# Smaller weight rows, unread padding and fewer full-precision passes in the routed expert blocks of a scan and mixture-of-experts kernel

## Chip, core and metric

The kernel runs on one core of a Trainium2 chip. The metric is the device time of one execution in microseconds (us); the median of three runs of the kernel before is 881.7 us (881.13 to 884.68). A core has TensorE (PE: matmuls), VectorE (DVE), ScalarE (ACT), GpSimd (POOL) and SyncE (SP), which here only issues transfers, and 16 DMA engines that they share. Each engine runs its own list of instructions in order; semaphores order them between engines.

## The reference

```python
x = x + xattn(ctx, layernorm(x))             # 2048 tokens, 512 features: a selective state-space scan
h = layernorm(x)
aff = sigmoid(h @ wa)                        # 16 experts
topk_p, topk_i = top_k(aff, 2);  topk_p /= sum(topk_p)
expert(e, h) = (gelu(h @ g[e] + gb[e]) * (h @ w1[e] + b1[e])) @ w2[e] + b2[e]   # 512 -> 256 -> 512
routed = sum over the two chosen e of topk_p * expert(e, h)
shared = sum of two experts that every token goes through
out = x + h + shared + routed
```

All is fp32. The change concerns `routed` alone.

## The kernel before

Up to about 406 us the kernel computes the projections and the scan, then, to about 596 us, gates, layer norms, the router and the two shared experts. The routed experts follow.

The 4096 pairs of token and expert are sorted by expert into NBLK = 47 blocks of 128 rows, and an expert's last block is filled up with padding rows. Blocks that no expert needs come first; they hold padding alone. The tables of the blocks lie in SBUF: `ids` (the tokens of its rows; padding has the numbers 2048 to 2175, which are spare rows of the scratch tensor `xn_dram` and of `out`), `row_w` (the routing weight of each row, 0 for padding), `blk_e` (the expert), `blk_load` (1 if the block has another expert than the block before it), `blk_slot` (which of four weight slots).

A block j is worked on by all engines, in a pipeline with a ring of four:
- SyncE, `load_up(j)` and `load_down(j)` (L387 to L402): reads expert, condition and slot from the tables into registers (L389 to L391) and issues a conditional DMA (L392) of 1 MB (up and gate weights, 128 rows of 8 KB) or 512 KB (down weights, rows of 4 KB). If the condition is 0, nothing is moved, but the semaphore is still raised. The order is load_down(j), load_up(j + 3), for j from 4 on. load_up(j + 3) first waits until the up product of block j - 1 is done, load_down(j) until the down product of block j - 4 is.
- GpSimd: `fetch` (L599) gathers the 128 token rows of a block from `xn_dram`, in the order of `ids`; later the indirect scatter-add of the block's result into `out` (L631). Scatter j waits until scatter j - 2 has landed, and, if a new expert begins, until scatter j - 1 has too.
- TensorE: turns the tokens (L1760), `up` (L1763 to L1776), turns the gated product (L1782), `down` (L1785 to L1795). `up` contracts 512 features in KC = 4 chunks of 128. KSPLIT = 2 of them are computed as three single-pass matmuls on values split into head and rest (L1446 to L1448), the others in full fp32 (L1774). Its order in step j is up(j + 1), turn_hidden(j), turn_tokens(j + 3), down(j - 1).
- ScalarE: `weight_head(j + 2)` (L906) and the heads and copies of the turned tokens (L898, L899), the Gelu (L910), the copy of the turned product (L915), and `block_result(j - 2)` (L919), which multiplies the result by `row_w`.
- VectorE: bias of the up product (L1385), rest of the tokens (L1377), bias of the result of block j - 2 (L1399), gated product (L1391), rest of the weights of block j + 2 (L1372).

The heads and rests lie in `acc_again`, the memory of `acc`, whose tiles hold the shared result until they are stored to `out` (L588). The biases of all experts are loaded in four transfers of 2 MB (L413 to L416), behind the first four up and four down loads.

Of the kernel before, what the change touches and what calls it, by code (L numbers as in the profile page):

```python
# [18 lines left out]
F32 = mybir.dt.float32  # L19
F32R = mybir.dt.float32r  # L20
I32 = mybir.dt.int32
U32 = mybir.dt.uint32
ALU = mybir.AluOpType
# [3 lines left out]
P = 128  # L27
# [16 lines left out]
AHEAD = 3  # L44
KSPLIT = 2
GROUP = NT // 2
# [6 lines left out]
def bass_xattn_scan_moe_kernel(nc, x, ctx_t, in_proj_t, conv_w, conv_b, x_proj_t, dt_proj_t, dt_b,  # L53
# [6 lines left out]
    with ExitStack() as ctx:  # L60
# [160 lines left out]
        with ExitStack() as listing:  # L221
            blk_val = listing.enter_context(nc.sbuf_tensor("blk_val", [P, 2, GROUP, 2 * NBLK], F32))
        blk_val_again = sb("blk_val_again", [P, 2 * GROUP * 2 * NBLK])
        AHEAD_OF_DOWN = (2 * SH * FC, 2 * SH * FC + 1)
        blk_val_all = blk_val[:].rearrange("p a g j -> p (a g j)")

# [6 lines left out]

        half_i = sb("half_i", [P, 2 * ((NBLK + 3) // 2)], I32)
        half_f = sb("half_f", [P, 2 * ((NBLK + 3) // 2)])
# [50 lines left out]
        uph_made upr_made xgr_made up_0 up_1 up_2 up_3 down_0 down_1 down_2 down_3 xg_0 xg_1 xg_2 xg_3 xgt_ready xgt_copied h_ready  # L286
        hb_ready hg_ready hy_ready hyt_ready hyt_copied o_ready yb_ready y_ready y_even y_odd
        """.split()
# [30 lines left out]
        def _(sp):  # L319
# [67 lines left out]

            def load(weights, r_weights, loaded, j, r):
                e = sp.value_load(blk_e[0:1, ds(j, 1)], min_val=0, max_val=E - 1)  # L389
                new = sp.value_load(blk_load[0:1, ds(j, 1)], min_val=0, max_val=1)  # L390
                slot_j = sp.value_load(blk_slot[0:1, ds(j, 1)], min_val=0, max_val=SLOTS - 1)  # L391
                sp.dma_start(weights[:, ds(slot_j, 1)], r_weights[ds(e, 1)].rearrange("e p n -> p e n"), cond=new).then_inc(s[f"{loaded}_{r}"], 16)  # L392

            def load_up(j, r):
                if not isinstance(j, int) or j >= SLOTS:
                    wait_apart(sp, s["h_ready"], j - SLOTS + 1)
                load(up_w, r_up, "up", j, r)

            def load_down(j, r):
                if not isinstance(j, int) or j >= SLOTS:  # L400
                    wait_apart(sp, s["o_ready"], j - SLOTS + 1)
                load(down_w, r_down, "down", j, r)  # L402

# [26 lines left out]
        def _(pool):  # L430
# [14 lines left out]
            pool.iota(tok_i[:], [[P, NT]], base=0, channel_multiplier=1).then_inc(s["consts_made"], 1)  # L445
            pool.iota(half_i[:], [[16, (NBLK + 3) // 2], [0, 2]], base=-16, channel_multiplier=0).then_inc(s["consts_made"], 1)
            pool.tensor_copy(iota_f[:], row_i[:, 0:48]).then_inc(s["consts_made"], 1)
            pool.wait_ge(s["consts_made"], 6)

            pool.dma_start(xn_dram[T:T + P, :], no_rows).then_inc(s["pad_stored"], 16)  # L450
            pool.dma_start(out[T:T + P, :], no_rows).then_inc(s["pad_stored"], 16)
            pool.tensor_copy(tok_f[:], tok_i[:]).then_inc(s["consts_made"], 1)
            pool.tensor_copy(half_f[:], half_i[:]).then_inc(s["consts_made"], 1)
            pool.wait_ge(s["consts_made"], 8)
# [131 lines left out]
            def store_base(t):  # L586
                pool.wait_ge(s["so_added"], t + 1)
                pool.dma_start(out[t * P:(t + 1) * P, :], acc[:, t]).then_inc(s["early_stored" if t < NT // 2 else "late_stored"], 16)  # L588

# [8 lines left out]
            def fetch(j):  # L598
                pool.indirect_dma_start(out=xg[:, j % RING], out_offset=None, in_=xn_dram,  # L599
                                        in_offset=bass.IndirectOffsetOnAxis(ids[:, j:j + 1], 0)).then_inc(  # L600
                                            s[f"xg_{j % RING}"], 16)
# [10 lines left out]
            for i in range(NBLK + BEHIND):  # L612
                if FIRST <= i and i + RING < NBLK:
                    pool.wait_ge(s["xgt_ready"], i + 1)
                    fetch(i + RING)
                j = i - BEHIND
                if j < 0:
                    continue
                if j == 0:
                    pool.wait_ge(s["early_stored"], 16 * NT // 2)  # L620
                    pool.wait_ge(s["late_stored"], 16 * NT // 2)
                pool.wait_ge(s["y_ready"], j + 1)
                if j >= 2:
                    pool.wait_ge(s["y_odd" if j % 2 else "y_even"], 16 * (j // 2))
                if 0 < j < 3:
                    pool.wait_ge(s["y_even" if j % 2 else "y_odd"], 16)
                elif j >= 3:

                    landed = pool.value_load(blk_wait[0:1, j:j + 1], min_val=16, max_val=16 * NBLK)
                    wait_apart(pool, s["y_even" if j % 2 else "y_odd"], landed)  # L630
                pool.indirect_dma_start(out=out, out_offset=bass.IndirectOffsetOnAxis(ids[:, j:j + 1], 0),  # L631
                                        in_=y_sb[j % RING], in_offset=None, compute_op=ALU.add).then_inc(
                                            s["y_odd" if j % 2 else "y_even"], 16)
# [5 lines left out]
        def _(act):  # L639
# [255 lines left out]
            def turn_tokens(j, half):  # L895
                act.wait_ge(s["xgt_ready"], j + 1)
                since(act, s["h_ready"], j - 1)
                act.copy(one_pass(xgt_head[:, half]), ps[:, 4 + half, 0:KSPLIT * P]).then_inc(s["xgt_copied"], 1)  # L898
                act.copy(xgt[:, half], ps[:, 4 + half, KSPLIT * P:D]).then_inc(s["xgt_copied"], 1)  # L899

            def weight_head(j, r, round_):

                slot_j = act.value_load(blk_slot[0:1, ds(j, 1)], min_val=0, max_val=SLOTS - 1)
                act.wait_ge(s[f"up_{r}"], 16 * (round_ + 1))
                since(act, s["h_ready"], j - 1)
                act.copy(one_pass(up_head[:, r % 2]), up_weights(slot_j, 0, KSPLIT)).then_inc(s["uph_made"], 1)  # L906

# [8 lines left out]

            def block_result(j, r):
                act.wait_ge(s["yb_ready"], j + 1)
                act.activation(y_sb[r], y_sb[r], ACT.Copy, scale=row_w[:, ds(j, 1)]).then_inc(s["y_ready"], 1)  # L919

            def step(j, round_, r):

                if not isinstance(j, int) or j + 2 < NBLK:
                    weight_head(j + 2, (r + 2) % RING, round_ + (r + 2) // RING)
                    turn_tokens(j + 2, r % 2)
                hidden_gate(j, r % 2)
                if not isinstance(j, int) or j >= 4:
                    block_result(j - 2, (r - 2) % RING)
                turn_hidden(j, r % 2)
                if isinstance(j, int) and j == 3:  # L930
                    block_result(0, 0)
                    block_result(1, 1)

# [3 lines left out]
            turn_tokens(1, 1)  # L937
            act.wait_ge(s["early_stored"], 16 * NT // 2)
            weight_head(0, 0, 0)
# [6 lines left out]
            for j in range((NBLK - 2) // RING * RING, NBLK):  # L946
                step(j, j // RING, j % RING)
            for j in range(NBLK - 2, NBLK):
                block_result(j, j % RING)


        @block.vector
        def _(dve):
# [433 lines left out]
            def hidden(j, half):  # L1387
                since(dve, s["hyt_ready"], j - 1)
                dve.wait_ge(s["hg_ready"], j + 1)
                dve.wait_ge(s["hb_ready"], j + 1)  # L1390
                dve.tensor_tensor(hy[:, half], hg[:, half], hb[:, half, F:2 * F], ALU.mult).then_inc(s["hy_ready"], 1)  # L1391

            def add_bias(j, r, round_):

                e = expert_of(j)
                if not isinstance(j, int) or j >= RING:
                    wait_apart(dve, s["y_odd" if r % 2 else "y_even"], 16 * (RING // 2 * round_ + r // 2 - 1))
                dve.wait_ge(s["o_ready"], j + 1)
                dve.tensor_tensor(y_sb[r], ps[:, 6 + r % 2], tile(b2_all, e), ALU.add).then_inc(s["yb_ready"], 1)  # L1399

            def step(j, round_, r):
# [3 lines left out]
                if not isinstance(j, int) or 1 < j < NBLK - 1:  # L1405
                    token_rest(j + 1, (r + 1) % 2)
                if not isinstance(j, int) or j >= 4:
                    add_bias(j - 2, (r - 2) % RING, round_ + (r - 2) // RING)
                hidden(j, r % 2)
                if isinstance(j, int) and j == 3:  # L1410
# [27 lines left out]
        def _(pe):  # L1438
# [346 lines left out]
            def down(j, r, round_):  # L1785
                slot_j = pe.value_load(blk_slot[0:1, ds(j, 1)], min_val=0, max_val=SLOTS - 1)
                pe.wait_ge(s["hyt_copied"], j + 1)
                pe.wait_ge(s[f"down_{r}"], 16 * (round_ + 1))
                if isinstance(j, int) and j == 0:
                    pe.wait_ge(s["so_added"], NT)  # L1790
                since(pe, s["yb_ready"], j - 1)
                for fc in range(FC):
# [90 lines left out]
```

## Time and profile before

| | us |
|---|---|
| median of 3 runs | 881.7 |
| profiled execution | 884.4 |
| its span | 882.3 |
| TensorE busy | 783.9 |
| VectorE busy | 660.8 |
| ScalarE busy | 557.5 |
| GpSimd busy | 550.5 |
| scan until | about 406 |
| routed blocks, first full-precision up product to the end | 596.4 to 882.3 |

Busy time leaves out register, branch, semaphore and DMA-issuing instructions: SyncE has no such row, and its load has to be read from the list of its issues and from the instructions of one line. The chain of work that ended last is followed back from the last instruction, at each step to what released it. A wait for several semaphores is put down to the one that came last. Line numbers (L392) are those of the kernel before.

### The profile page before, as it was taken

How to read it: one execution, taken by the hardware profiler on the slowest of the kernel's cores; microseconds unless marked ns; L12 is line 12 of the kernel's file. 1: busy time of each engine (PE TensorE's matmuls, PEld its weight loads, DVE VectorE, ACT ScalarE, POOL GpSimd, SP SyncE). 2: the span in 40 equal slices, each digit the busy share in tenths (PEclk: the TensorE clock that was granted, in tenths of full speed). 3: DMA queues.
4: the chain of work that ended last, by engine and by line, in shares of the span. 5: the costliest groups of instructions: out<-in, count | busy, mean ns of one | idle time of the engine just before them, and what ended most of it. 6: DMA issues, size and time to landing. Idle time of an engine off the chain costs nothing.

```text
span 882.3 us, 16042 instructions
## 1 busy us (share of the span) xinstructions
PE 783.9 (89%) x4358; PEld 589.2 (67%) x4359; DVE 660.8 (75%) x859; ACT 557.5 (63%) x931; POOL 550.5 (62%) x347
## 2 busy tenths in 40 slices
PE   6963799999999988997899999999999998999992
PEld 3622688888888878886777778886555554555551
DVE  4999999999999998999586759544655555556651
ACT  3896899999999999994333431024555554545541
POOL 9651399989999999997815560211444543546532
PEclk9975899999999999999799999999999999999996
DMA  6010311212141122101220121366577867678753
GB/s 182 1 55 0 108 52 58 60 49 61 50 155 49 54 61 92 59 14 49 95 96 1 49 102 42 129 253 275 121 163 226 235 175 223 154 211 205 180 143 48
DMA packets 35384, 95.57 MB, mean 108 GB/s; under 512 B 7760, under 2 KB 8272, under 8 KB 32000
## 3 DMA queue, kind: packets, MB, share of 16 engines
q1 hardware_dynamic: 23360, 65.50, 21.6%
q0 software_dynamic: 11968, 29.37, 15.6%
q8 instruction: 30, 0.49, 0.2%
q14 instruction: 26, 0.21, 0.1%
HBM read 122.24 MB, written 21.36 MB: 163 GB/s over the span
## 4 chain that ended last, share of the span: by engine, by line
PE 43%; DMA 17%; DVE 17%; POOL 9%; issue 7%; ACT 5%; POOLq 1%; DVEq 0%; SPq 0%; ACTq 0%
DVE r L1060 12%; DMA out<-sb_sb,ids 9%; DMA out<-sg,ids 8%; PE ps L1446 6%; PE ps L1448 6%; PE ps L1447 6%; PE ps L1549 5%; POOL r L526 5%; PE ps L1572 5%; PE ps L1550 3%; PE ps L1774 3%; PE ps L1793 2%; DVE r L963 1%; POOL r L599 1%; ACT mem L765 1%
## 5 line engine op out<-in xcount | busy, mean ns | idle before, releaser
L526 POOL TENSOR_TENSOR r<-r,mem 128x1024 f32<-128x1024 f32 x126 | 295.4, 2380 | 34.8 <-DVE r L1060 34.2
L1060 DVE TENSOR_TENSOR_SCAN r<-r,ps 128x1024 f32<-128x1024 f32 x128 | 286.7, 2276 | 9.7 <-issue 9.1
L750 ACT ACTIVATE r<-mem,nega 128x511 f32<-128x511 f32 x256 | 166.9, 714 | 1.8 <-DVE r L1060 1.7
L1549 PE MATMUL ps<-ident,mem 128*128 128x128 f32 x768 | 130.3, 279 | 28.4 <-DVE r L1060 21.7
L1572 PE MATMUL ps<-ident,r 128*128 128x128 f32 x1024 | 132.6, 273 | 1.5 <-POOL r L526 1.3
L765 ACT ACTIVATE mem<-mem,b_turned 128x512 f32<-128x512 f32 x192 | 124.7, 715 | 8.7 <-PE ps L1550 8.3
L1549 PEld LDWEIGHTS ps<-ident,mem 128*128 128x128 f32 x768 | 87.2, 142 | 53.8 <-issue 52.8
L1572 PEld LDWEIGHTS ps<-ident,r 128*128 128x128 f32 x1024 | 115.8, 141 | 2.3 <-POOL r L526 1.8
L1550 PE MATMUL ps<-mem 128*128 128x128 f32 x512 | 99.7, 277 | 0.0
L1793 PE MATMUL ps<-mem 128*128 x188 | 92.2, 615 | 1.8 <-ACT mem L915 1.0
L1446 PE MATMUL ps<-split 128*128 128x512 f32 x216 | 88.2, 408 | 4.8 <-DVE split L1134 2.3
L1774 PE MATMUL ps<-r,picked 128*128 x188 | 88.3, 592 | 0.0
L631 POOL DMA_INDIRECT out<-sg,ids x24 | 40.6, 1693 | 72.4 <-DMA out<-sg,ids 29.6
L1448 PE MATMUL ps<-split 128*128 128x512 f32 x216 | 85.0, 394 | 0.0
L1447 PE MATMUL ps<-split 128*128 128x512 f32 x216 | 85.0, 394 | 0.0
L1550 PEld LDWEIGHTS ps<-mem 128*128 128x128 f32 x512 | 78.1, 193 | 0.0
L631 POOL DMA_INDIRECT out<-sb_sb,ids x23 | 38.1, 1656 | 61.4 <-DMA out<-sb_sb,ids 32.0
L1372 DVE TENSOR_TENSOR acc_again<-r,acc_again 128x1024 fp32r<-128x1024 f32 x47 | 57.6, 1225 | 20.4 <-issue 20.0
L906 ACT CAST acc_again<-r 128x1024 fp32r x47 | 49.1, 1046 | 32.7 <-issue 21.9
L599 POOL DMA_INDIRECT r<-xn_scratch,ids x47 | 49.6, 1055 | 31.8 <-PE ps L1760 19.2
L915 ACT COPY mem<-ps 128x256 f32<-128x256 f32 x47 | 17.5, 372 | 67.9 <-PE ps L1782 67.7
L825 ACT ACTIVATE sg<-ps,sbg_sb 128x512 f32<-128x512 f32 x16 | 11.0, 688 | 71.0 <-PE ps L1448 71.0
(205 smaller groups left out, 1304.8 us busy)
## 6 DMA issues: line engine op xcount, KB each, us to landing
r<-in_r_up SPq DMA_DIRECT2D x47, 1024.0 KB
mem<-in_r_down SPq DMA_DIRECT2D x47, 512.0 KB
mem<-cm_rows SPq DMA_DIRECT2D x64, 256.0 KB, 3.3
mem<-in_r_b SPq DMA_DIRECT2D x4, 2048.0 KB, 15.1
out<-acc POOLq DMA_DIRECT2D x17, 256.0 KB, 3.2
r<-in_x SPq DMA_DIRECT2D x4, 1024.0 KB, 4.9
xn_scratch<-r SPq DMA_DIRECT2D x16, 256.0 KB, 2.7
mem<-in_ctx_t SPq DMA_DIRECT2D x4, 512.0 KB, 7.7
```

Of the source, the lines that this page charges most:

```text
L526: pool.tensor_tensor(state[:, k % 2, ec:ec + 2], state[:, k % 2, ec:ec + 2], c, ALU.mult).then_inc(s["weighed"], 1)
L750: act.activation(decay[:, k % 2, ec, 1:L], delta[:, b, ec, 1:L], ACT.Exp, scale=nega[:, ec, n:n + 1]).then_inc(s["decay_ready"], 1)
L765: act.activation(dbu_t[:, k % 2, lt], du_t[:, t], ACT.Copy, scale=b_turned[:, t, k % DS:k % DS + 1]).then_inc(s["dbut_made_a"], 1)
L1060: dve.tensor_tensor_scan(state[:, half, ec:ec + 2].rearrange("p e l -> p (e l)"), decay[:, half, ec:ec + 2].rearrange("p e l -> p (e l)"), ...
L1446: pe.matmul(to, one_pass(l_head), one_pass(r_head), start=(first and i == 0), stop=False)
L1447: pe.matmul(to, one_pass(l_head), one_pass(r_rest), start=False, stop=False)
L1448: mm = pe.matmul(to, one_pass(l_rest), one_pass(r_head), start=False, stop=(last and i == n - 1))
L1549: pe.transpose(ps[:, ec, lt * P:(lt + 1) * P], dbu_t[:, k % 2, lt, ec * P:(ec + 1) * P], ident[:])
L1550: pe.matmul(ps[:, ec, (LT - 1) * P:LT * P], du_t[:, k // DS * LT + LT - 1, ec * P:(ec + 1) * P], b_diag[k % 2], start=True, stop=True).the ...
L1572: mm = pe.matmul(ps[:, Y_BANK + lt, ec * P:(ec + 1) * P], state[:, k % 2, ec, lt * P:(lt + 1) * P], ident[:], is_transpose=True, start=Fal ...
L1774: mm = pe.matmul(ps[:, r % 2], xgt[:, r % 2, (kc - KSPLIT) * P:(kc - KSPLIT + 1) * P], up_weights(slot_j, kc, kc + 1), start=False, stop=( ...
L1793: mm = pe.matmul(ps[:, 6 + r % 2], hyt[:, r % 2, fc * P:(fc + 1) * P], down_weights(slot_j, fc), start=(fc == 0), stop=(fc == FC - 1))
```

## The change

- `load` takes a list of parts: load_up issues four DMAs of one chunk each (128 rows of 2 KB), load_down two (128 rows of 2 KB), all with the same condition, registers and semaphore. Those who wait for the weights wait for 16 x 4 or 16 x 2.
- `fetch` has a bounds check: padding rows are not read, and the rows of `xg` keep what they held.
- VectorE multiplies by `row_w`: the gated product and the bias each take it in a fused operation. `block_result` and its semaphore are gone; the bias add raises `y_ready` itself.
- In VectorE's step the gated product stands before the bias add of block j - 2.
- KSPLIT = 3: three chunks in single passes, one in full fp32. The heads and rests are longer by half.
- ScalarE's first weight head waits until 12 tiles of the shared result are stored, not 8. Some tables share memory.

```diff
-KSPLIT = 2
+KSPLIT = 3
...
-            def load(weights, r_weights, loaded, j, r):
+            def load(parts, loaded, j, r):
+
                 e = sp.value_load(blk_e[0:1, ds(j, 1)], min_val=0, max_val=E - 1)
                 new = sp.value_load(blk_load[0:1, ds(j, 1)], min_val=0, max_val=1)
                 slot_j = sp.value_load(blk_slot[0:1, ds(j, 1)], min_val=0, max_val=SLOTS - 1)
-                sp.dma_start(weights[:, ds(slot_j, 1)], r_weights[ds(e, 1)].rearrange("e p n -> p e n"), cond=new).then_inc(s[f"{loaded}_{r}"], 16)
+                for weights, r_weights in parts:
+                    sp.dma_start(weights[:, ds(slot_j, 1)], r_weights[ds(e, 1)].rearrange("e p n -> p e n"), cond=new).then_inc(s[f"{loaded}_{r}"], 16)
...
-                load(up_w, r_up, "up", j, r)
+                load([(up_w[:, :, kc * 2 * F:(kc + 1) * 2 * F], r_up[:, :, kc * 2 * F:(kc + 1) * 2 * F]) for kc in range(KC)], "up", j, r)
...
-                load(down_w, r_down, "down", j, r)
+                load([(down_w[:, :, fc], r_down[:, :, fc * D:(fc + 1) * D]) for fc in range(FC)], "down", j, r)
...
-                                        in_offset=bass.IndirectOffsetOnAxis(ids[:, j:j + 1], 0)).then_inc(
+                                        in_offset=bass.IndirectOffsetOnAxis(ids[:, j:j + 1], 0),
+                                        bounds_check=T - 1, oob_is_err=False).then_inc(
...
-                act.wait_ge(s[f"up_{r}"], 16 * (round_ + 1))
+                act.wait_ge(s[f"up_{r}"], 16 * KC * (round_ + 1))
...
-            def block_result(j, r):
-                act.wait_ge(s["yb_ready"], j + 1)
-                act.activation(y_sb[r], y_sb[r], ACT.Copy, scale=row_w[:, ds(j, 1)]).then_inc(s["y_ready"], 1)
-
...
-            act.wait_ge(s["early_stored"], 16 * NT // 2)
+            act.wait_ge(s["early_stored"], 16 * (NT - LT))
...
-                dve.tensor_tensor(hy[:, half], hg[:, half], hb[:, half, F:2 * F], ALU.mult).then_inc(s["hy_ready"], 1)
+                dve.scalar_tensor_tensor(out=hy[:, half], in0=hg[:, half], scalar=row_w[:, ds(j, 1)], in1=hb[:, half, F:2 * F],
+                                         op0=ALU.mult, op1=ALU.mult).then_inc(s["hy_ready"], 1)
...
-                dve.tensor_tensor(y_sb[r], ps[:, 6 + r % 2], tile(b2_all, e), ALU.add).then_inc(s["yb_ready"], 1)
+                dve.scalar_tensor_tensor(out=y_sb[r], in0=tile(b2_all, e), scalar=row_w[:, ds(j, 1)], in1=ps[:, 6 + r % 2],
+                                         op0=ALU.mult, op1=ALU.add).then_inc(s["y_ready"], 1)
...
+                hidden(j, r % 2)
                 if not isinstance(j, int) or j >= 4:
                     add_bias(j - 2, (r - 2) % RING, round_ + (r - 2) // RING)
-                hidden(j, r % 2)
...
-                pe.wait_ge(s[f"down_{r}"], 16 * (round_ + 1))
+                pe.wait_ge(s[f"down_{r}"], 16 * FC * (round_ + 1))
```

## Rows read from the trace of the kernel before

**Rows 1.** The chain that ended last, in time: start, us, engine, tile, line.

```profile
653.97 1.72 PE ps L1774 x4
656.34 1.72 PE ps L1793 x4
659.46 1.72 PE ps L1774 x4
...
741.21 9.65 DMA out<-sg,ids
...
863.73 4.87 DMA out<-sg,ids
871.25 1.56 POOL out L631
```

**Rows 2.** The page's chain of work, shares of the span by engine.

```profile
PE 43%; DMA 17%; DVE 17%; POOL 9%; issue 7%; ACT 5%; POOLq 1%; DVEq 0%; SPq 0%; ACTq 0%
```

**Rows 3.** SyncE's issues in order of time: start us, us, engine, line, operation.

```profile
562.29 7.82 SPq L392 DMA_DIRECT2D r<-in_r_up  x4
...
582.71 0.84 SPq L413 DMA_DIRECT2D mem<-in_r_b  x2
...
610.79 0.08 SPq L392 DMA_DIRECT2D mem<-in_r_down  x1
...
648.37 0.35 SPq L392 DMA_DIRECT2D r<-in_r_up  x1
...
843.34 0.09 SPq L392 DMA_DIRECT2D r<-in_r_up  x1
```

**Rows 4.** Waits of SyncE from 610 to 845 us: in total, times, longest.

```profile
SPq L304 <- PE ps L1793: 5.5, 3, 3.2
SPq L304 <- PE ps L1774: 3.8, 8, 0.9
```

**Rows 5.** ScalarE in order of time: the weight head of block 46.

```profile
849.38 1.04 ACT L906 CAST acc_again<-r 128x1024 fp32r x1 [0.46 <-issue]
```

**Rows 6.** Line L389, a register read: ns min/median/max, first and last start.

```profile
L389 SPq TENSOR_LOAD <-blk_e x94: 263/272/1352, 560.0 to 850.8; - x94
```

**Rows 7.** Line L392, the conditional DMA, in the same columns.

```profile
L392 SPq FUSED_REGOPS  x94: 183/183/189, 561.9 to 853.0; - x94
L392 SPq ALU_OP  x94: 32/37/48, 562.1 to 853.2; - x94
...
L392 SPq DMA_DIRECT2D mem<-in_r_down x47: 83/93/357, 572.2 to 853.4; - x47
```

**Rows 8.** Line L1774 on TensorE's sequencer, in the same columns.

```profile
L1774 PEldq FUSED_REGOPS  x94: 46/56/65, 592.5 to 855.2; - x94
```

**Rows 9.** Packets, MB and share of 16 engines: 210 to 230 us, 406 to 414 us.

```profile
q1 hardware_dynamic: 699, 1.28, 21.0%
...
q1 hardware_dynamic: 125, 1.02, 36.5%
```

**Rows 10.** Stretch 640 to 700 us: busy PE, PEld, DVE, ACT, POOL, clock, DMA share, GB/s.

```profile
640.00:700.00 60.00, 58.24 (x210) 34.14 (x209) 34.09 (x54) 32.00 (x65) 29.36 (x22) 1.00 0.78 202
```

**Rows 11.** Groups from 600 to 840 us: busy us, mean ns | idle before, releasers.

```profile
L1372 DVE TENSOR_TENSOR acc_again<-r,acc_again 128x1024 fp32r<-128x1024 f32 x42 | 51.5, 1225 | 18.2 <-issue 17.8
L906 ACT CAST acc_again<-r 128x1024 fp32r x42 | 43.9, 1045 | 21.9 <-issue 21.0 <-DMA r<-in_r_up 0.9
...
L910 ACT ACTIVATE mem<-mem 128x256 f32<-128x256 f32 x43 | 18.5, 429 | 0.0
...
L1377 DVE TENSOR_TENSOR blk_val_again<-ps,blk_val_again 128x256 fp32r<-128x256 f32 x42 | 17.4, 413 | 0.0
...
L919 ACT ACTIVATE sb_sb<-sb_sb,row_w 128x512 f32<-128x512 f32 x20 | 14.4, 722 | 14.6 <-DVE sb_sb L1399 14.4
```

**Rows 12.** VectorE in order of time: the first bias of an up product.

```profile
598.92 0.69 DVE L1385 TENSOR_TENSOR mem<-ps,mem 128x512 f32<-128x512 f32 x1 [3.19 <-DMA mem<-in_r_b]
```

**Rows 13.** Line L631, the scatter, from 660 to 882 us: issue to landing.

```profile
DMA to landing us min/median/max: 4.5/5.2/10.1
```

More of the change, by code:

```diff
@@ L221, in bass_xattn_scan_moe_kernel @@
         with ExitStack() as listing:
-            blk_val = listing.enter_context(nc.sbuf_tensor("blk_val", [P, 2, GROUP, 2 * NBLK], F32))
-        blk_val_again = sb("blk_val_again", [P, 2 * GROUP * 2 * NBLK])
+            blk_val_all = listing.enter_context(nc.sbuf_tensor("blk_val", [P, 4 * KSPLIT * P], F32))
+        blk_val_again = sb("blk_val_again", [P, 4 * KSPLIT * P])
+        blk_val = blk_val_all[:, 0:2 * GROUP * 2 * NBLK].rearrange("p (a g j) -> p a g j", a=2, g=GROUP)
         AHEAD_OF_DOWN = (2 * SH * FC, 2 * SH * FC + 1)
-        blk_val_all = blk_val[:].rearrange("p a g j -> p (a g j)")
         def raw_hidden(i):
@@ L232, in raw_hidden @@
             return sy_raw[:, i % (SH * FC)]
-        half_i = sb("half_i", [P, 2 * ((NBLK + 3) // 2)], I32)
+        half_i = row_i[:, 0:2 * ((NBLK + 3) // 2)]
         half_f = sb("half_f", [P, 2 * ((NBLK + 3) // 2)])
@@ L286, in bass_xattn_scan_moe_kernel @@
         uph_made upr_made xgr_made up_0 up_1 up_2 up_3 down_0 down_1 down_2 down_3 xg_0 xg_1 xg_2 xg_3 xgt_ready xgt_copied h_ready
-        hb_ready hg_ready hy_ready hyt_ready hyt_copied o_ready yb_ready y_ready y_even y_odd
+        hb_ready hg_ready hy_ready hyt_ready hyt_copied o_ready y_ready y_even y_odd
         """.split()
@@ L445, in _ @@
             pool.iota(tok_i[:], [[P, NT]], base=0, channel_multiplier=1).then_inc(s["consts_made"], 1)
-            pool.iota(half_i[:], [[16, (NBLK + 3) // 2], [0, 2]], base=-16, channel_multiplier=0).then_inc(s["consts_made"], 1)
             pool.tensor_copy(iota_f[:], row_i[:, 0:48]).then_inc(s["consts_made"], 1)
+            pool.wait_ge(s["consts_made"], 5)
+            pool.iota(half_i, [[16, (NBLK + 3) // 2], [0, 2]], base=-16, channel_multiplier=0).then_inc(s["consts_made"], 1)
             pool.wait_ge(s["consts_made"], 6)
@@ L452, in _ @@
             pool.tensor_copy(tok_f[:], tok_i[:]).then_inc(s["consts_made"], 1)
-            pool.tensor_copy(half_f[:], half_i[:]).then_inc(s["consts_made"], 1)
+            pool.tensor_copy(half_f[:], half_i).then_inc(s["consts_made"], 1)
             pool.wait_ge(s["consts_made"], 8)
@@ L587, in store_base @@
                 pool.wait_ge(s["so_added"], t + 1)
-                pool.dma_start(out[t * P:(t + 1) * P, :], acc[:, t]).then_inc(s["early_stored" if t < NT // 2 else "late_stored"], 16)
+                pool.dma_start(out[t * P:(t + 1) * P, :], acc[:, t]).then_inc(s["early_stored" if t < NT - LT else "late_stored"], 16)
             for t in range(NT - LT):
@@ L619, in _ @@
                 if j == 0:
-                    pool.wait_ge(s["early_stored"], 16 * NT // 2)
-                    pool.wait_ge(s["late_stored"], 16 * NT // 2)
+                    pool.wait_ge(s["early_stored"], 16 * (NT - LT))
+                    pool.wait_ge(s["late_stored"], 16 * LT)
                 pool.wait_ge(s["y_ready"], j + 1)
@@ L898, in turn_tokens @@
                 act.copy(one_pass(xgt_head[:, half]), ps[:, 4 + half, 0:KSPLIT * P]).then_inc(s["xgt_copied"], 1)
-                act.copy(xgt[:, half], ps[:, 4 + half, KSPLIT * P:D]).then_inc(s["xgt_copied"], 1)
+                act.copy(xgt[:, half, 0:D - KSPLIT * P], ps[:, 4 + half, KSPLIT * P:D]).then_inc(s["xgt_copied"], 1)
             def weight_head(j, r, round_):
                 slot_j = act.value_load(blk_slot[0:1, ds(j, 1)], min_val=0, max_val=SLOTS - 1)
-                act.wait_ge(s[f"up_{r}"], 16 * (round_ + 1))
+                act.wait_ge(s[f"up_{r}"], 16 * KC * (round_ + 1))
                 since(act, s["h_ready"], j - 1)
@@ L926, in step @@
                 hidden_gate(j, r % 2)
-                if not isinstance(j, int) or j >= 4:
-                    block_result(j - 2, (r - 2) % RING)
                 turn_hidden(j, r % 2)
-                if isinstance(j, int) and j == 3:
-                    block_result(0, 0)
-                    block_result(1, 1)
             act.wait_ge(s["blocks_ready"], 3)
@@ L947, in _ @@
                 step(j, j // RING, j % RING)
-            for j in range(NBLK - 2, NBLK):
-                block_result(j, j % RING)
         @block.vector
@@ L1787, in down @@
                 pe.wait_ge(s["hyt_copied"], j + 1)
-                pe.wait_ge(s[f"down_{r}"], 16 * (round_ + 1))
+                pe.wait_ge(s[f"down_{r}"], 16 * FC * (round_ + 1))
                 if isinstance(j, int) and j == 0:
                     pe.wait_ge(s["so_added"], NT)
-                since(pe, s["yb_ready"], j - 1)
+                since(pe, s["y_ready"], j - 1)
                 for fc in range(FC):
```

## Prediction

> **What bounds the kernel now.** I read the chain of work that ended last first, in order of time. From 596 us to 670 us it consists of TensorE alone: a 1.72 us step of the full-precision up products, then one of the down products, again and again, with 5.49 us from one block to the next [rows 1] (653.97 to 659.46). From 670 us on it changes hands: the links are the transfers of the scatter-add into `out`, 4.9 to 9.7 us each [rows 1]. A scatter waits for the one two before it and, where a new expert begins, for the one just before it, so they go out almost one by one. Over the whole routed stage (596 to 871 us, 47 blocks) a block costs 5.9 us. The share of the page's chain says the same: TensorE 43%, DMA 17% [rows 2]. So TensorE (5.5 us per block) and the scatters share the bound.
>
> The third thing to read is a queue that the chain doesn't show: SyncE, which issues the weights. In the list of its issues, load_down(4) goes out at 610.79 us and load_up(46) at 843.34 us [rows 3]. Between them lie 79 further loads, 232.6 us, so 2.94 us from one to the next. Did it wait? The waits of SyncE in that stretch add up to 5.5 + 3.8 = 9.3 us [rows 4]. Without them a load costs (232.6 - 9.3) / 79 = 2.83 us of SyncE's own time, 5.65 us for the two loads of a block. That is as long as TensorE's block. SyncE works without a pause through the whole stage, and it has to do so for all 47 blocks, though only 16 of them have a new expert: a load whose condition is false still reads three registers and goes through the same instructions. It is not late yet. Load_up(46) is issued at 843.34 us and ScalarE takes its weights at 849.38 us [rows 3, 5], 6 us later.
>
> **What a load costs on SyncE.** Three register reads of a table, 0.27 us each at the median [rows 6], with their own address arithmetic and range tests make up most of the 2.83 us. The line of the dma_start itself (L392) has, for each DMA, one FUSED_REGOPS of 183 ns, one ALU_OP of 37 ns, and the DMA instruction, 93 ns where nothing is loaded and about 0.35 us where it is [rows 3, 7]. Their counts are all 94 for 94 DMAs. The last FUSED_REGOPS starts at 853.0 us and its DMA at 853.4 us [rows 7], so with the small gaps one DMA costs about 0.48 us.
>
> **The change, part by part.**
>
> (a) Loads in 2 KB rows. Each load_up becomes four dma_starts and each load_down two: four more per block. The register reads stay one set per load. Is the address arithmetic repeated for each part? No row shows several conditional DMAs after one another on SyncE. The nearest is TensorE's sequencer: two matmuls of one block that differ only in a constant offset from the same slot register have 94 FUSED_REGOPS for 94 uses [rows 8], one for each instruction. I take the repeat: 4 x 0.48 = 1.92 us per block. The other end is the bare instruction and a gap, 0.15 us each. Where a load is real, its four more DMAs cost (0.35 - 0.09) = 0.26 us each more, 16 times in 47 blocks: 4 x 0.26 x 16 / 47 = 0.35 us per block. SyncE's block becomes 5.65 + 1.92 + 0.35 = 7.92 us (low end 5.65 + 0.60 + 0.35 = 6.6 us). It can't go below zero: nothing of the old load is removed.
>
> The page "DMA: Bandwidth & Descriptors" of the Trainium skill, section "Anatomy of one DMA", puts the sequencer's dispatch of a DMA at about 50 ns. By that figure the four would add 0.2 us and the time would come out near 890 us; the row of L392 disagrees, with 93 ns for the instruction alone [rows 7] and its address work ahead of it.
>
> For the transfers themselves: a 2 KB packet of the broadcast rows took 0.21 x 20 us x 16 / 699 = 96 ns, and an 8 KB packet of `x` 0.365 x 8 us x 16 / 125 = 374 ns [rows 9]. Four small ones are 384 ns, so the bytes cost the same; a gain can only come to others that share the engines.
>
> (b) Padding not gathered. 47 x 128 - 4096 = 1920 of 6016 rows are skipped. By an estimate seven blocks are wholly unused (47 less the 4096 / 128 = 32 full ones and half a block for each of 16 experts), and they come first. That takes some 4 MB off engines that are 78% busy [rows 10]. It lightens the gathers, which nobody waits for, and perhaps the scatters.
>
> (c) Three of four up chunks in single-pass products. TensorE's block is now 1.72 (one down) + 1.72 (two full-precision chunks) + 1.40 (six single passes, 658.06 to 659.46) + 0.65 (turns) = 5.49 us [rows 1]. One chunk goes from 0.86 to 3 x 0.233 = 0.70 us, so 5.33 us, 0.16 us less; over 47 blocks 7.5 us at most. The price is on others: ScalarE's head copy grows from 1.05 to 1.57 us, VectorE's rest from 1.23 to 1.84 us, the token parts from 0.41 to about 0.6 us [rows 11]. Both engines have room: VectorE is busy 34 of 60 us [rows 10].
>
> (d) Routing weight by VectorE. ScalarE loses 0.72 us per block and a step between VectorE and the scatter [rows 11]. The bias add now stands behind the gated product, so that waits for a scatter no longer hold TensorE up; but it no longer fills the time in which VectorE waits for the Gelu. The two fused operations cost what the plain ones do, give or take 0.1 us; hidden by the same slack.
>
> (e) The opening. Four up loads start at 562.29 us, the down loads follow, and the biases are issued at 582.71 us, as soon as they may [rows 3]. Then VectorE waits 3.19 us for them, until 598.92 us [rows 12]. The twelve + four further DMAs take 16 x 0.48 + 4 x 0.26, about 8.7 us, of which some 3 us were idle time: the biases come 5.5 us later and the block loop on SyncE starts near 613 instead of 608.6 us. The wait for twelve stored tiles instead of eight costs nothing: they are stored long before 586 us.
>
> **The sum.** From 613 us SyncE has 40 pairs to go until load_up(46) is out: 40 x 7.92 = 317 us, so 930 us. Behind it stand now 39 us (843.3 to 882.3), 6 of them slack; the remaining 33 us are the last blocks and scatters. They lose about 2 us, because scatters no longer pile up: 31 us. Span 930 + 31 = 961 us; the profiled execution of before took 2.1 us more than its span (884.4 to 882.3) and was 2.7 us over the median of 881.7 us. So 961 + 2.1 - 2.7, about **960 us**. TensorE then waits some 2.6 us in each block, and the gains of (b), (c) and (d) all fall into that wait: SyncE is late next, whoever else is faster.
>
> **Rivals.**
>
> R1, address arithmetic shared between the parts of a load: 0.15 us per further DMA, SyncE's block 6.6 us, 610 + 264 + 31 = 905 us, less half a microsecond. For it: the slot and expert registers are the same. Against it: [rows 8].
>
> R2, the other side: SyncE doesn't decide, since a load's 2.83 us hides waits, and the rest gets its gains. Then TensorE's 5.33 us per block is the pace, and scatter landings, 4.5 to 10.1 us [rows 13], all come near the short end, because a small row of a scatter no longer stands behind an 8 KB row: 596 + 47 x 5.33 + 20 = 867 us, with 1 us of opening 868 us. It decides only if the four further DMAs and their real cost stay under about 0.5 us per block (today's 5.9 us minus 5.65, and 10 us of lead spread over 40 blocks). The real part alone is 0.35 us.
>
> The same page, section "Queues, rings and completion order", says that an engine drains a whole packet, typically 9 to 17 descriptors, before it turns to another queue. By that rule smaller rows would not shorten a scatter's wait, and R2 would keep most of its 7 to 9.7 us links; the rows here can't tell the two apart.
>
> R3, ScalarE and VectorE become the loop: head copy 1.57, token copies 0.8, Gelu 0.43 and rest 1.84 [rows 11], the bias add 0.69 [rows 12], the gated product with half its columns at about 0.4, and some 0.4 for a register read, in a row, closed through TensorE's 2.95 us up product; with latencies I estimate 5.9 us per block. 596 + 47 x 5.9 + 20 = 893 us. Needs SyncE below 5.9 us.
>
> R4, worse than my sum: in TensorE's waits the granted clock, 1.00 in the stage now [rows 10], falls, or a real load in four parts lands so late that the blocks slip: 975 us and up.
>
> **How the numbers follow.** The forecast (SyncE at about 7.9 us per block) gets 0.72, R1 0.12, R2 0.05, R3 0.04, R4 0.07. Range 893 to 985 us: it takes in R1, R3 and the low part of R4, and leaves out R2 and an extreme R4. A difference of 0.5% is about what a measurement of this kernel can tell from none: faster 0.04, same 0.02, slower 0.94.
>
> **What the profile would show.** Right: from about 613 us on the spacing of real pairs of loads on SyncE near 8 us, FUSED_REGOPS of the dma_start line counted 282 times, 6 for each of 47 blocks, hardly a wait on SyncE; TensorE waiting for VectorE's rest of the up weights, which waits for ScalarE's head copy, which waits for nothing but the load; the chain of work through SyncE or "issue"; scatters landing in some 5 us and off the chain. The up products in 2.95 us. Wrong: 94 FUSED_REGOPS for 282 DMAs (R1); SyncE waiting for h_ready in every block (R2, R3); half the granted clock over long stretches (R4). What would overturn all of it: if SyncE's 2.83 us per load shrank with smaller DMAs.

## The result, and the profile after

The changed kernel takes 966.9 us (median of 4 runs, 965.4 to 968.1), the kernel before 881.4 us beside it: 1.098 times as long, 95% interval 1.095 to 1.101. The forecast was 960 us, slower.

The chain of work that ended last, on the profile page of the changed kernel, in shares of the span. SPq is SyncE's list of instructions:

```profile
PE 28%; SPq 22%; DVE 19%; issue 13%; POOL 7%; ACT 5%; DMA 3%; DVEq 1%; POOLq 0%; ACTq 0%
```

In [rows 2] SPq had 0% and DMA 17%. SyncE has come into the chain, and the scatters have left it. The dma_start line of SyncE (now L394; ns min/median/max, first and last start), its issues in order of time, and its waits from 605 to 960 us, all of the changed kernel:

```profile
L394 SPq FUSED_REGOPS  x282: 2/168/433, 561.6 to 938.3; - x141
L394 SPq ALU_OP  x282: 3/33/354, 561.8 to 938.5; - x141
L394 SPq DMA_DIRECT2D r<-in_r_up x188: 3/83/579, 562.0 to 929.3; - x188
```

```profile
588.50 0.84 SPq L415 DMA_DIRECT2D mem<-in_r_b  x2
...
615.07 1.46 SPq L394 DMA_DIRECT2D r<-in_r_up  x4
619.14 0.54 SPq L394 DMA_DIRECT2D mem<-in_r_down  x2
...
641.11 0.55 SPq L394 DMA_DIRECT2D mem<-in_r_down  x2
644.06 2.81 SPq L394 DMA_DIRECT2D r<-in_r_up  x4
649.80 0.57 SPq L394 DMA_DIRECT2D mem<-in_r_down  x2
652.80 1.46 SPq L394 DMA_DIRECT2D r<-in_r_up  x4
656.70 0.54 SPq L394 DMA_DIRECT2D mem<-in_r_down  x2
...
927.89 1.48 SPq L394 DMA_DIRECT2D r<-in_r_up  x4
```

```profile
SPq L304 <- PE ps L1769: 7.4, 1, 7.4
```

FUSED_REGOPS stands 282 times for 282 DMAs: the address arithmetic is made again for every part (94 for 94 DMAs in [rows 7]). Four skipped DMAs of one load take 1.46 us from the start of the first to the end of the last, so 0.46 us from one to the next; where the four move data they take 2.5 to 2.8 us. From load_down(4) at 619.14 us to load_up(46) at 927.89 us it is 308.8 us for 79 loads, 3.91 us each, 7.8 us per block, where [rows 3] gave 5.9. SyncE's only wait in all that time is one of 7.4 us before 619 us.

Who waits now? A group of the page (busy us, mean ns, idle before it, what ended it), and TensorE's stretch from 700 to 760 us (busy PE, PEld, DVE, ACT, POOL, granted clock, DMA share, GB/s):

```profile
L910 ACT CAST acc_again<-r 128x1536 fp32r x47 | 69.1, 1473 | 103.8 <-DMA r<-in_r_up 80.6
```

```profile
700.00:760.00 60.00, 49.92 (x167) 29.76 (x168) 32.21 (x40) 19.63 (x36) 24.09 (x17) 0.88 0.60 152
```

ScalarE stands 80.6 us before its weight heads for the up loads, against 0.9 us in [rows 11]. TensorE is busy 50 of 60 us, and part of that at the lower level of its clock: 0.88 granted, against 1.00 in [rows 10]. The lower clock doesn't change SyncE's pace: SyncE waits for TensorE nowhere between 619 us and load_up(46).

### The profile page after: what moved, and what is told of

It is laid out like the page before. It is cut to its first block, busy times and chain, and to the rows that moved or that the text cites. A ratio compares the mean times of both kernels' runs of the same rounds, so it can differ in the third digit from the quotient of the medians.

```text
span 965.6 us, 16837 instructions
## 1 busy us (share of the span) xinstructions
PE 803.2 (83%) x4405; PEld 602.0 (62%) x4406; DVE 699.0 (72%) x859; ACT 545.9 (57%) x884; POOL 563.1 (58%) x347
## 4 chain that ended last, share of the span: by engine, by line
PE 28%; SPq 22%; DVE 19%; issue 13%; POOL 7%; ACT 5%; DMA 3%; DVEq 1%; POOLq 0%; ACTq 0%
DVE r L1053 11%; SPq L394 10%; PE ps L1544 5%; POOL r L529 5%; PE ps L1567 5%; SPq L390 4%; SPq L391 4%; SPq L392 4%; PE ps L1441 3%; PE ps L1443 3%; PE ps L1442 3%; PE ps L1545 3%; POOL split L534 1%; DMA mem<-in_r_b 1%; DVE r L956 1%
## 5 line engine op out<-in xcount | busy, mean ns | idle before, releaser
L910 ACT CAST acc_again<-r 128x1536 fp32r x47 | 69.1, 1473 | 103.8 <-DMA r<-in_r_up 80.6
L635 POOL DMA_INDIRECT out<-sg,ids x24 | 44.7, 1864 | 108.7 <-issue 52.0
L1788 PE MATMUL ps<-mem 128*128 x188 | 104.3, 684 | 2.6 <-ACT mem L919 1.8
L1384 DVE SCALAR_TENSOR_TENSOR mem<-mem,row_w 128x256 f32<-128x256 f32 x47 | 22.8, 485 | 110.6 <-ACT mem L914 108.5
L635 POOL DMA_INDIRECT out<-sb_sb,ids x23 | 44.9, 1951 | 89.2 <-issue 50.4
L1365 DVE TENSOR_TENSOR acc_again<-r,acc_again 128x1536 fp32r<-128x1536 f32 x47 | 82.6, 1758 | 16.5 <-issue 16.1
L1441 PE MATMUL ps<-acc_again,blk_val_again 128*128 128x512 f32 x141 | 64.0, 454 | 17.4 <-DVE blk_val_again L1370 15.5
```

What stands on the lines that cost most here:

```text
L1441: pe.matmul(to, one_pass(l_head), one_pass(r_head), start=(first and i == 0), stop=False)
L1788: mm = pe.matmul(ps[:, 6 + r % 2], hyt[:, r % 2, fc * P:(fc + 1) * P], down_weights(slot_j, fc), start=(fc == 0), stop=(fc == FC - 1))
```

## The experiments

**Each load in one DMA again, all other edits kept.**

```diff
-                load([(up_w[:, :, kc * 2 * F:(kc + 1) * 2 * F], r_up[:, :, kc * 2 * F:(kc + 1) * 2 * F]) for kc in range(KC)], "up", j, r)
+                load([(up_w, r_up)], "up", j, r)
-                load([(down_w[:, :, fc], r_down[:, :, fc * D:(fc + 1) * D]) for fc in range(FC)], "down", j, r)
+                load([(down_w, r_down)], "down", j, r)
```

> The changed kernel with each weight load in one DMA again (rows of 8 KB and 4 KB); all its other edits stay. SyncE theory: a load costs 2.8 us of SyncE again, 5.65 us per block, so the time falls from 967 to between 865 and 893 us: 868 us if TensorE's 5.33 us per block sets the pace, 880 us if SyncE's 5.65 us does, 893 us if the loop through ScalarE and VectorE (5.9 us) does. Rival theory, the longer head and rest and the new order on VectorE cause the slowdown: the time stays above 940 us.

Measured: 894.7 us (893.6 to 895.2), ratio to before 1.018 (1.015 to 1.021). So the split costs 72 us (966.9 to 894.7). The kernel before took 879.1 us beside this run, so 15.6 us are still there with the split gone: the rest of the change is itself a loss.

**The split alone, in the kernel before.** The edit is the `load` of the changed kernel with its counts of semaphores, nothing else.

> The kernel before with the split of the loads alone (four and two DMAs of 2 KB rows). SyncE theory: 7.9 us per block on SyncE whatever the others do, so the time is that of the changed kernel, 955 to 968 us. Rival theory (ScalarE and VectorE cause the slowdown): 880 to 895 us.

Measured: 967.7 us (963.3 to 968.8), ratio 1.100 (1.096 to 1.103), the same as the whole change. SyncE's issues in it:

```profile
617.53 0.54 SPq L394 DMA_DIRECT2D mem<-in_r_down  x2
...
927.71 1.48 SPq L394 DMA_DIRECT2D r<-in_r_up  x4
```

310.2 us for 79 loads, 3.93 us each, with other heads, another order on VectorE and all padding gathered: SyncE's list alone makes the kernel as slow as the whole change does.

**One further DMA per block instead of four.** The up load in two parts of 4 KB rows, the down load whole.

```diff
-                load(up_w, r_up, "up", j, r)
+                load([(up_w[:, :, c * 2 * 2 * F:(c + 1) * 2 * 2 * F], r_up[:, :, c * 2 * 2 * F:(c + 1) * 2 * 2 * F]) for c in range(2)], "up", j, r)
```

> The kernel before with the up load in two DMAs (rows of 4 KB), the down load in one: one further DMA per block instead of four. SyncE theory: 5.65 + 0.48 + 0.09 = 6.2 us per block on SyncE, 40 pairs in 249 us from 609 us on and 31 to 33 us behind them: about 890 us, 1% over the kernel before. If SyncE has room for one more DMA per block: 881 to 884 us.

Measured: 896.4 us (894.3 to 898.6), ratio 1.020 (1.017 to 1.023). Load_down(4) goes out at 611.10 us and load_up(46) at 854.82 us: 3.09 us per load, 6.2 us per block as expected, and SyncE waits 0.2 us in all that time. The time came out 6 us later than the 890 us: the start was 2 us later, the loads took 5 us less, and what follows the last up load took 40 us and not 31 to 33.

**The instructions without the DMAs.** The kernel before, transfers as they were; each load reads a table register twice more and doesn't use it.

```diff
                 slot_j = sp.value_load(blk_slot[0:1, ds(j, 1)], min_val=0, max_val=SLOTS - 1)
+                sp.value_load(blk_load[0:1, ds(j, 1)], min_val=0, max_val=1)
+                sp.value_load(blk_load[0:1, ds(j, 1)], min_val=0, max_val=1)
```

> The kernel before, transfers untouched, but each load on SyncE reads one table register twice more, to no use: four reads more per block, at 0.27 us and about 0.2 us of range test each (0.48 us, the price of a further DMA). SyncE theory: about 7.6 us per block, 40 pairs in 304 us from 612 us on and 36 us behind them: 945 to 960 us without one DMA or small row more. Rival theory (DMA count, rows or queues cost the time): no change, 877 to 882 us.

Measured: 972.6 us (970.0 to 974.6), ratio 1.104 (1.099 to 1.109). Its chain, SyncE's issues and SyncE's waits from 610 to 960 us:

```profile
PE 25%; SPq 25%; DVE 18%; issue 12%; POOL 7%; DMA 5%; ACT 5%; DVEq 0%; POOLq 0%; ACTq 0%
```

```profile
619.04 0.08 SPq L394 DMA_DIRECT2D mem<-in_r_down  x1
...
936.62 0.09 SPq L394 DMA_DIRECT2D r<-in_r_up  x1
```

```profile
SPq L304 <- PE ps L1776: 7.4, 1, 7.4
```

4.02 us per load. A read costs (8.04 - 5.65) / 4 = 0.60 us, where I had 0.48; that is 14 us over 40 pairs. With the start at 619 instead of 612 us it makes 972 us and not 945 to 960. No DMA, no byte and no row is added here, and the kernel is as slow as with the split. What costs is the length of SyncE's list.

**Small rows, one DMA.** The weights lie in DRAM as chunk, row, column, so that one DMA has rows of 2 KB.

```diff
-        "r_down": _rows(i["ffn_rw2"], FC).reshape(E, P, FC * D),
+        "r_down": i["ffn_rw2"].reshape(E, FC, P, D),
...
-                    sp.dma_start(weights[:, ds(slot_j, 1)], r_weights[ds(e, 1)].rearrange("e p n -> p e n"), cond=new)
+                    sp.dma_start(weights[:, ds(slot_j, 1)].rearrange("p o k n -> p (o k) n"), r_weights[ds(e, 1)].rearrange("e k p n -> p (e k) n"), cond=new)
```

> As the changed kernel, with rows of 2 KB, but each load one single DMA: the weights lie in DRAM so that one DMA has 512 (up) or 256 (down) rows of 2 KB. It tells the rows from the number of DMAs. SyncE theory: within 1% of the kernel with 8 KB rows in one DMA, 865 to 893 us. If the small rows let the scatters through sooner, their median landing falls from 5.2 to under 4.9 us and the longest from 10 to under 8 us, and it is some us faster than that kernel; if the size of the rows is what costs, it is near 960 us.

Measured: 895.4 us (893.5 to 895.7), ratio 1.018 (1.015 to 1.021), against 894.7 us with 8 KB rows in the same run. The landings of the scatters from 660 to 882 us (us min/median/max), first with 8 KB and 4 KB rows, then with 2 KB rows:

```profile
DMA to landing us min/median/max: 4.9/6.0/9.9
```

```profile
DMA to landing us min/median/max: 4.4/5.6/8.8
```

They are a little shorter, by less than was expected of small rows, in one profile each, and the time is the same. The size of the rows neither costs nor brings anything that can be measured here. Both kernels have the scatters at 1% of their chain, so this doesn't show what shorter landings would bring where scatters are on the path.

**Two chunks in single passes instead of three**, on top of the single DMAs (KSPLIT = 2; the size of `blk_val_again` written as a number).

> The changed kernel with single DMAs and with two of four chunks in single passes instead of three. Loop theory (the longer head on ScalarE and rest on VectorE close a loop of 6.0 us per block): the loop loses about 0.9 us and TensorE's 5.5 us is the pace again, 872 to 882 us. If the order on VectorE alone makes the loop: 890 us or more.

Measured: 878.7 us (877.2 to 881.2), ratio 1.000 (0.998 to 1.002).

**Three chunks, but VectorE's old order.**

```diff
-                hidden(j, r % 2)
                 if not isinstance(j, int) or j >= 4:
                     add_bias(j - 2, (r - 2) % RING, round_ + (r - 2) // RING)
+                hidden(j, r % 2)
```

> The changed kernel with single DMAs and three chunks in single passes, but on VectorE the bias add of block j - 2 stands before the gated product, as in the kernel before. Loop theory: the bias add (0.75 us and a register read) fills the wait for the Gelu again instead of standing behind it, so the loop gets 0.5 to 0.9 us shorter: 872 to 885 us. If the order doesn't matter: 892 to 897 us.

Measured: 879.6 us (878.9 to 881.5), ratio 1.000 (0.999 to 1.002).

Either edit takes the 15 us away, so neither the third chunk nor the order costs them alone: together they do. The kernel with both (and single DMAs) shows why, in the order of time, once on ScalarE and VectorE, and in its waits from 600 to 850 us:

```profile
654.29 1.47 ACT L910 CAST acc_again<-r 128x1536 fp32r x1 [1.09 <-issue]
655.67 0.47 ACT L902 CAST blk_val_again<-ps 128x384 fp32r<-128x384 f32 x1
656.04 0.27 ACT L903 COPY picked<-ps 128x128 f32<-128x128 f32 x1
656.19 0.43 ACT L914 ACTIVATE mem<-mem 128x256 f32<-128x256 f32 x1
```

```profile
656.80 0.50 DVE L1384 SCALAR_TENSOR_TENSOR mem<-mem,row_w 128x256 f32<-128x256 f32 x1 [1.79 <-ACT mem L914]
```

```profile
DVE mem L1384 <- ACT mem L914: 50.7, 42, 2.7
PEld ps L1441 <- ACT picked L903: 24.0, 13, 2.1
PE ps L1441 <- DVE blk_val_again L1370: 18.5, 17, 1.7
```

The Gelu (L914) stands behind the longer head and token copies, VectorE waits for it with nothing else in hand, and the bias add and the 1.76 us rest come after. Then TensorE waits for tokens. VectorE's wait alone isn't what costs: with two chunks it is just as long (53.5 us from 610 to 850 us). What differs is TensorE, busy 59.5 of the 60 us from 640 us on with two chunks and 54.7 with three.

**The Gelu first**, in that same kernel.

```diff
             def step(j, round_, r):
 
+                hidden_gate(j, r % 2)
                 if not isinstance(j, int) or j + 2 < NBLK:
                     weight_head(j + 2, (r + 2) % RING, round_ + (r + 2) // RING)
                     turn_tokens(j + 2, r % 2)
-                hidden_gate(j, r % 2)
```

> The changed kernel with single DMAs (three chunks in single passes, new order on VectorE), but on ScalarE the Gelu of block j stands before the weight head and token copies of block j + 2. Loop theory: the Gelu no longer waits for 1.5 + 0.5 us of copies, VectorE's wait for it (50 us in 240) goes, and the pace is SyncE's 5.65 or TensorE's 5.33 us per block with the scatters: 868 to 880 us. If the Gelu's place doesn't matter: 892 to 897 us.

Measured: 880.7 us (875.4 to 888.5), ratio 1.000 (0.997 to 1.003). A third way to open the loop; it ends at the same 880 us.

**The Gelu first, and the old order on VectorE.**

> As the one with the Gelu first, but with the old order on VectorE (bias add before the gated product). With both waits in place of one another: if the Gelu is early, the bias add ahead of the product only puts 0.75 us and a wait for a scatter in front of it, so this is 0 to 5 us slower than the one with the new order.

Measured: 880.8 us (877.1 to 885.0), ratio 1.001 (0.998 to 1.004): no difference that can be measured.

**The Gelu first, and shorter register reads on SyncE.**

```diff
-                e = sp.value_load(blk_e[0:1, ds(j, 1)], min_val=0, max_val=E - 1)
+                e = sp.value_load(blk_e[0:1, ds(j, 1)])
```

and the same for the other two.

> As the one with the Gelu first, and SyncE's register reads have no range test (some 0.15 us less each, 0.9 us per block: 4.7 us instead of 5.65). If SyncE still holds that kernel up in places: 3 to 8 us faster than it. If the scatters or TensorE do: within 2 us of it.

Measured: 876.7 us (874.1 to 884.2), ratio 0.9956 (0.993 to 0.998), 4 us under the one with range tests. SyncE's waits from 610 to 960 us in it, and then GpSimd's from 610 to 850 us:

```profile
SPq L304 <- PE ps L1769: 27.7, 38, 1.8
SPq L304 <- PE ps L1788: 17.2, 18, 3.5
```

```profile
POOL out L635 <- DMA out<-sb_sb,ids: 50.5, 11, 6.9
POOL out L635 <- DMA out<-sg,ids: 33.1, 10, 5.7
```

Now SyncE waits 45 us and the scatters are next. The chains, first with the Gelu first, then with the shorter reads as well:

```profile
PE 38%; SPq 15%; DVE 15%; issue 10%; ACT 9%; POOL 7%; DMA 3%; DVEq 0%; POOLq 0%; ACTq 0%
```

```profile
PE 38%; DMA 18%; DVE 17%; POOL 10%; issue 8%; ACT 5%; POOLq 1%; DVEq 0%; SPq 0%; ACTq 0%
```

SyncE's list has left the chain, so it did hold up the kernel with the Gelu first. The single times of the two overlap; from the ten of each the gain is about 1.5 to 5.7 us.

Load_down(4) goes out at 609.10 us and load_up(46) at 832.84 us: 2.83 us per load with its waits, (223.7 - 44.9) / 79 = 2.26 us without. In the four variants at 879 to 881 us the same two issues are 225.6 to 228.0 us apart, 5.7 to 5.8 us per block, with 5 to 7 us of waits on TensorE. They agree in their time, but not in what holds them. The chain with two chunks:

```profile
PE 49%; DVE 15%; ACT 11%; POOL 8%; issue 7%; SPq 4%; DMA 2%; DVEq 1%; ACTq 1%; POOLq 0%
```

There TensorE, busy 59.5 of 60 us, sets the pace with the 5.5 us of its block. With three chunks TensorE's block is shorter (5.33 us by the prediction) and SyncE's 5.65 us show: SPq has 14% of the chain with the old order and 15% with the Gelu first, but only 8% with both, where DMA has 9%. So the common 880 us are several bounds that lie close together, and that SyncE is the bound is shown by a run only for the kernel with the Gelu first.

**Both loads of a block behind one set of reads.** This was to keep the DMAs and shorten the list. Up and down load of block j wait together for `o_ready`, which the down load waited for alone.

```diff
+            def load_both(j, r):
+                wait_apart(sp, s["o_ready"], j - SLOTS + 1)
+                load(ups + downs, j, r)
...
-                    load_down(RING * jj + r, r)
-                    load_up(RING * jj + r + AHEAD, (r + AHEAD) % RING)
+                    load_both(RING * jj + r + AHEAD, (r + AHEAD) % RING)
```

In the changed kernel (six DMAs kept):

> The changed kernel with all six DMAs of 2 KB rows kept, but up and down load of a block issued together after one set of register reads. SyncE theory: 2.83 + 5 x 0.46 + 0.35 = about 5.5 us per block on SyncE instead of 7.85, so the time falls to that of the changed kernel with single DMAs, 890 to 900 us. If the number of DMAs or of rows as such costs the time (queues, landings) and not SyncE's instructions, it stays above 950 us.

Measured: 1232.7 us, ratio 1.402 (1.397 to 1.406). In the kernel before:

> The kernel before with up and down load issued together after one set of register reads: 3.3 us per block on SyncE instead of 5.65. If SyncE was only about to become late in the kernel before: 876 to 882 us, no change. If SyncE already held it up in places: under 874 us.

Measured: 1111.9 us, ratio 1.264 (1.261 to 1.266). Waits of SyncE in the latter from 610 to 1100 us:

```profile
SPq L304 <- PE ps L1798: 328.0, 42, 12.6
```

Both missed, and they say nothing on the question they were made for. SyncE waits 328 us for the down product (L1798). By the order of the lists (no run took the new wait away alone) it closes a loop of one block: the up load of block j waits for down(j - 4); ScalarE's head for block j, and behind it the Gelu of block j - 2, wait for that load; down(j - 3) stands on TensorE behind the turn of that very product; and the next load waits for down(j - 3). So no block would overlap the next one's load any more. The question was answered by the reads without DMAs instead.

## Why the prediction was right, step by step

- *SyncE had no room.* Right, and it gives the whole result. The split alone gives 1.100, the register reads alone 1.104, one DMA more per block 1.020.
- *0.48 us for each further DMA.* It took 0.46 us. The doubtful step, that the address arithmetic is repeated for each part, held: 282 for 282. That was read from TensorE's 94 uses [rows 8], a thin sign: the trace has 188 matmuls and 188 weight loads on that line, so 94 is one for each matmul of the program, of which the trace shows two parts each, and TensorE's sequencer need not have spoken for SyncE's. R1 is out. The 50 ns that the prediction takes from the Trainium skill ("DMA: Bandwidth & Descriptors", "Anatomy of one DMA") stand there for a DMA that GpSimd issues, not SyncE; no run here shows them.
- *7.92 us per block.* It took 7.8 us: 308.8 us for 79 loads. Load_up(46) was forecast for 930 us and went out from 927.9 to 929.4 us.
- *The start, 613 us instead of 608.6 us.* Too early. Load_down(4) moved from 610.8 to 619.1 us, 8.4 us and not 4.4 us. The biases came 5.8 us later, as forecast (582.71 to 588.50 us), and VectorE got them at 603.47 instead of 598.92 us. But SyncE itself then stood 7.4 us before load_up(6), until block 2's up product was done. I had left that wait out.
- *31 us behind the last up load.* The term was 7 us too small: it took 37.7 us from the load's first DMA (927.9 to 965.6), 38.9 us before. I had taken off the 6 us of slack between load_up(46) and ScalarE's head of its weights, and 2 us for scatters that no longer pile up. But the head started at 931.5 us, 3.6 us after the load's first DMA, and what followed took 34.1 us, where it had been 32.9 us.
- *The sum.* The span came out at 965.6 us, not 961: the loop on SyncE started 4 us later than forecast, its 40 pairs took 6 us less, and the end took 7 us more. That these misses partly cancel is luck. The other 2 us lie between span and median: I had put the median 0.6 us below the span, and it is 1.3 us above.
- *TensorE's gain of 0.16 us per block and the lighter gathers fall into the wait.* Right: the whole change and the split alone cannot be told apart (966.9 and 967.7 us).
- *R3, the loop through ScalarE and VectorE, 893 us.* It was there, hidden by SyncE: 894.7 us with single DMAs. Its two parts, the longer copies and the bias add behind the product, were named in (c) and (d), and each was costed there as hidden by slack. Each costs nothing that can be measured, alone; both together cost 1.8%.
- *R2, the other side, 868 us.* Not reached by any kernel here. With the loop open and SyncE eased it is 877 us, with the scatters' transfers at 18% of the chain, as before the change (17%). The landings, which R2 wanted near the short end, had medians of 6.0 and 5.6 us with large and small rows.
- *R4, the granted clock.* It did fall, to 0.88 to 0.96 in the stage, while TensorE waited, and SyncE's loads kept their pace.

The gathers of padding are still packets, but empty ones. Queues from 573 to 590 us, when three of the first blocks are gathered, which hold padding alone:

```profile
q0 software_dynamic: 240, 0.00, 0.7%
```

That is 80 packets for the 128 rows of a gather. The kernel before, which reads all rows, has 400 packets and 1.31 MB on this queue from 568 to 583 us, which by the bytes are four gathers and one store of 256 KB: 80 packets each too. So the packets stay and the bytes go. The empty ones took 0.007 x 17 us x 16 / 240 = 8 ns each on average. Whether leaving them out moves the time was not tried alone; with two chunks and single DMAs it is part of a kernel that ties with the one before.

## What to carry to other kernels

An engine that only issues transfers has no busy time on the profile page, but its list can be the bound: take the distance between its issues, subtract its waits, and set that beside the time of a block. A conditional DMA that moves nothing still costs its full share of instructions, so a split into parts must be paid for in every block, not only where something is loaded. And two edits that each use up another engine's slack are to be costed together: here each was free alone, and both together cost 1.8%. Kernels that tie in time need not have the same bound: the chain of each tells.

## What the runs showed of the hardware that was not expected

A register read on SyncE, with its address and range test, cost 0.60 us in the run with reads alone, more than a further skipped DMA (0.46 us). Leaving the range tests out made a load 2.26 instead of 2.83 us. A gather whose 128 rows are all dropped by the bounds check still leaves 80 packets, without bytes and of 8 ns each on average.
